# Eight PSUM banks in the ring, and the attention's output summed over head pairs in SBUF

## What is computed

```python
h   = layernorm(x)
# 1: causal attention, 16 heads of 64
qkv = h @ W_qkv + b_qkv
a   = softmax(Q K^T / 8 + causal) V        # per head
a   = a @ W_out + b_out                    # sum over 16 heads = 8 pairs of heads
# 2: two layers of a local transformer, 8 heads of 64, window 64
for l in range(2):
    q, k, v = split(shift(y) @ wqkv[l])    # q, k: l2norm, scale, rotary (x8 on q)
    y = y + local_attention(q, k, v) @ wo[l]
    y = y + (a_ * gelu(g)) @ w2[l] + b2[l] # a_, g from layernorm(shift(y)) @ w1[l]
out = x + a + y
```

## Time and profile before

| | |
|---|---|
| median of 3 runs | 3653.97 us (3653.33 to 3658.05) |
| the profiled execution | 3660.12 us, its span 3658.1 us |
| busy share of the span | PE 87%, DVE 53%, ACT 47%, POOL 28% |
| granted TensorE clock, mean | 0.977 |
| one pass of the loop | 225.0 to 227.9 us, mean 226.4 |

### The profile page before, as it was taken

One profiled execution on the slowest core, in us unless ns is written; L12 is line 12 of the kernel. 1 busy time (PEld: TensorE's weight loads), 2 busy tenths in 40 slices (PEclk: granted clock), 3 DMA queues, 4 the chain that ended last, 5 costly groups with the idle time before them and its releaser, 6 DMA issues.

```text
span 3658.1 us, 95074 instructions
## 1 busy us (share of the span) xinstructions
PE 3187.2 (87%) x34560; PEld 2107.2 (58%) x34560; DVE 1923.1 (53%) x6830; ACT 1704.6 (47%) x3140; POOL 1007.9 (28%) x987
## 2 busy tenths in 40 slices
PE   6888888888888898888988889888898888988897
PEld 4555565555655555555655556555565565555655
DVE  5554554546546464464645546455464464645544
ACT  4444444544444454444544445444454444444543
POOL 4140422404224041240413305133051330513221
PEclk9999999999999999999999999999999999999999
DMA  3000000000000000000000000000000000000000
GB/s 83 8 2 4 8 2 11 2 5 8 2 11 2 5 8 2 11 2 5 8 2 11 2 11 2 2 11 2 11 2 2 11 2 11 2 2 8 2 7 4
DMA packets 41905, 26.37 MB, mean 7 GB/s; under 512 B 13058, under 2 KB 40620, under 8 KB 41388
## 3 DMA queue, kind: packets, MB, share of 16 engines
q1 hardware_dynamic: 41388, 19.56, 1.9%
HBM read 14.96 MB, written 4.19 MB: 5 GB/s over the span
## 4 chain that ended last, share of the span: by engine, by line
PE 64%; issue 10%; DVE 9%; POOL 7%; ACT 4%; DVEq 0%; POOLq 0%; ACTq 0%
PE bank L1175 6%; PE bank L1221 6%; PE bank L1090 6%; PE bank L1207 4%; PE bank L1269 4%; PE bank L1083 3%; POOL rnorm L712 3%; PE bank L1286 3%; PE bank L1251 3%; PE bank L1199 3%; PE bank L1233 2%; PE bank L1309 2%; PE bank L1319 2%; PE bank L1084 2%; PE bank L1085 2%
## 5 line engine op out<-in xcount | busy, mean ns | idle before, releaser
L940 DVE CUSTOM_DVE_ANT_0 bank<-bank,future 128x128 f32<-128x128 f32 (+3 forms) x1024 | 467.9, 527 | 262.6 <-PE bank L1135 262.1
L955 DVE CUSTOM_DVE_ANT_0 bank<-bank,band 128x192 f32<-128x192 f32 x1024 | 330.7, 394 | 248.8 <-PE bank L1154 247.2
L712 POOL TENSOR_TENSOR rnorm<-ssc,minus_half 128x8 f32<-128x8 f32 x256 | 426.5, 1666 | 21.3
L1175 PE MATMUL bank<-Qa,Ka 64*128 64x512 f32 (+3 forms) x2048 | 397.7, 472 | 2.7 <-DVE scratch L997 2.7
L793 ACT ACTIVATE probs<-bank 128x512 f32<-128x512 f32 (+1 forms) x768 | 347.5, 532 | 106.3 <-PE bank L1184 104.7
L1221 PEld LDWEIGHTS bank<-Va,probs 128*64 128x64 f32 x10240 | 327.8, 141 | 104.0 <-issue 88.9
L994 DVE TENSOR_TENSOR scratch<-bank,rope_t 128x512 f32<-128x512 f32 x256 | 176.2, 688 | 355.0 <-ACT scratch L826 217.2
L1221 PE MATMUL bank<-Va,probs 128*64 128x65 f32 x10240 | 361.6, 228 | 0.1
L701 POOL TENSOR_TENSOR lrstd<-lvar,minus_half 128x4 f32<-128x4 f32 x32 | 32.4, 1012 | 1181.6 <-DVE lvar L1018 1181.6
L826 ACT ACTIVATE scratch<-bank 128x512 f32<-128x512 f32 x256 | 153.1, 598 | 437.9 <-PE bank L1269 321.6
L710 POOL TENSOR_SCALAR ssc<-ss 128x8 f32<-128x8 f32 x256 | 95.1, 372 | 855.4 <-DVE ss L1002 843.4
(11 more groups left out here) (153 smaller groups left out, 7011.1 us busy)
## 6 DMA issues: line engine op xcount, KB each, us to landing
x_res<-in_L_attn_x SPq DMA_DIRECT2D x16, 256.0 KB, 2.9
x_rows<-in_L_attn_x SPq DMA_DIRECT2D x16, 256.0 KB, 3.2
out<-yT SPq DMA_DIRECT2D x16, 256.0 KB, 2.3
Lqkv<-in_L_ffn_wqkv SPq DMA_DIRECT2D x2, 768.0 KB, 5.1
rope_t<-in_rope SPq DMA_DIRECT2D x8, 128.0 KB, 4.9
Kf<-in_L_attn_W_qkv SPq DMA_DIRECT2D x1, 768.0 KB, 7.8
Qf<-in_L_attn_W_qkv SPq DMA_DIRECT2D x1, 768.0 KB, 9.4
Lw<-in_L_ffn_w SPq DMA_DIRECT2D x2, 341.0 KB
```

Source lines behind the costliest of these rows:

```text
L712: g.tensor_tensor(rnorm[s][:, :], ssc[:, :], minus_half[:, :], ALU.pow).then_inc(rnorm_ready.sem, 1)
L940: ins = v.tensor_tensor_reduce(psum.bank(i, task, (u, j))[:, at:at + n], psum.bank(i, task, (u, j))[:, at:at + n], future[:, SEQ - n:SEQ], ...
L955: ins = v.tensor_tensor_reduce(psum.bank(i, task, (u, j))[:, k * BAND:(k + 1) * BAND], psum.bank(i, task, (u, j))[:, k * BAND:(k + 1) * BAND],
L1175: mm(bank[j][:, at:end], Ka[p % 2][HALF[j], tile(k)], Qa[p % 2][HALF[j], queries], start=True, stop=False)
```

## The change

- `RING` is 8: every bank belongs to the ring, also in the planner.
- `a_out` claims a bank of the ring for every pair, and its matmul stands alone (`start` and `stop` both set). DVE reads it: for p = 0 it writes bank + bias into the new tile aT_sum, for p = 1 to 6 it adds the bank to aT_sum in place, for p = 7 it writes bank + aT_sum into aT. Before each of these it waits for its own last one (through the read semaphore of that bank), and for p = 7 for the previous `out` on PE, as `a_end` did.
- `a_end`, `out_acc` and the semaphores out_ready and aT_ready are gone. `a_ot` on ACT waits until the last `a_out` filled its bank, where it waited for out_ready; `out` on PE waits until DVE has read the bank of a_out(7).
- The planner has `a_out` with a step of 0.75 on DVE and one bank, and makes a new order.

```diff
-RING = 7
+RING = 8
 BANKS = {...
+         "a_out": 1, ...
-    "a_out": (0.85, [], 0),
-    "a_end": (0.0, [("dve", 0.75, 0.0)], 0),
+    "a_out": (0.85, [("dve", 0.75, 0.0)], 1),
...
-                    elif kind == "a_end":
-                        psum.wait_filled(dve, i, ("out",), "t", before_it(i, task, ("out",)))
-                        dve.sem_inc(carried["dve"], 1)
-                        dve.wait_ge(out_ready.sem, out_ready.now(i, ("a_out", PAIRS - 1), "a"))
-                        v.tensor_scalar(aT, out_acc[:, :], bout[:, 0:1], None, ALU.add).then_inc(aT_ready.sem, 1)
+                    elif kind == "a_out":
+                        p = task[1]
+                        if p == 0:
...
+                            psum.raise_read(v.tensor_scalar(aT_sum, psum.bank(i, task, "u")[:, :], bout[:, 0:1], None, ALU.add), i, task, "u")
+                        else:
+                            other = ("a_out", p - 1)
+                            psum.wait_read(dve, i, other, "u", before_it(i, task, other))
+                            dve.sem_inc(carried["dve"], 1)
+                            if p == PAIRS - 1:
+                                psum.wait_filled(dve, i, ("out",), "t", before_it(i, task, ("out",)))
+                                dve.sem_inc(carried["dve"], 1)
+                            psum.wait_filled(dve, i, task, "u")
+                            psum.raise_read(v.tensor_tensor(aT if p == PAIRS - 1 else aT_sum, psum.bank(i, task, "u")[:, :], aT_sum, ALU.add), i, task, "u")
...
-                        if p == 0:
-                            pe.wait_ge(aT_ready.sem, aT_ready.value(i, ("a_end",), "a", before_it(i, task, ("a_end",))))
-                        mm(out_acc[:, :], Wout[:, p, :], OaT[:, :], start=(p == 0),
-                           stop=(p == PAIRS - 1)).then_inc(out_ready.sem, 1)
+                        bank = psum.claim(pe, i, task, "u")
+                        psum.raise_filled(mm(bank[:, :], Wout[:, p, :], OaT[:, :], start=True, stop=True), i, task, "u")
...
                     elif kind == "out":
-                        pe.wait_ge(aT_ready.sem, aT_ready.now(i, ("a_end",), "a"))
+                        other = ("a_out", PAIRS - 1)
+                        psum.wait_read(pe, i, other, "u", before_it(i, task, other))
+                        pe.sem_inc(carried["pe"], 1)
```

More of the change, by code:

```diff
@@ L52 @@
            ("f_v", 3), ("f_qt", 3), ("f_kt", 3)]
-RING = 7
+RING = 8
 BANKS = {"f_first": 1, "a_proj": 2, "a_v": 1, "a_neg": 1, "a_ot": 1, "f_q": 1, "f_k": 1, "f_v": 1, "f_qt": 1, "f_kt": 1, "f_neg": 1, "f_ot": 1,
-         "f_wo": 1, "f_mean": 1, "f_var": 1, "f_rep": 1, "f_gate": 3, "f_up": 1, "f_down": 1, "out": 1, "xt": 1,
+         "a_out": 1, "f_wo": 1, "f_mean": 1, "f_var": 1, "f_rep": 1, "f_gate": 3, "f_up": 1, "f_down": 1, "out": 1, "xt": 1,
          "a_max": 6, "f_max": 4, "a_st": 6, "f_st": 4, "a_pv": 1, "f_pv": 1}
@@ L113 @@
 A_BEGUN = [task for r in range(-1, PAIRS // 2) for task in attention_round(r)]
-A_REST = [task for r in range(PAIRS // 2, PAIRS + 1) for task in attention_round(r)] + [("a_end",)]
+A_REST = [task for r in range(PAIRS // 2, PAIRS + 1) for task in attention_round(r)]
 def heavy_tasks(l):
@@ L147, in needs @@
         "a_out": lambda: [("a_ot", *at)],
-        "a_end": lambda: [("a_out", PAIRS - 1)],
         "f_first": lambda: [("norm",)],
@@ L161, in needs @@
         "xt": lambda: [("norm",), ("a_proj", PAIRS - 1), ("a_v", PAIRS // 2 - 1, 1)],
-        "out": lambda: [("f_down", DEPTH - 1), ("a_end",)]}.get(kind, lambda: [])()]
+        "out": lambda: [("f_down", DEPTH - 1), ("a_out", PAIRS - 1)]}.get(kind, lambda: [])()]
 def by_ready_time(streams, rotary, pair):
@@ L237 @@
 assert in_order(("norm",), ("f_first",), ("xt",), ("a_proj", 0)) and in_order(("a_proj", PAIRS - 1), ("xt",))
-assert in_order(("a_v", PAIRS // 2 - 1, 1), ("xt",)) and in_order(("a_end",), ("out",)) and in_order(("a_end",), ("a_out", 0))
+assert in_order(("a_v", PAIRS // 2 - 1, 1), ("xt",)) and in_order(("a_out", PAIRS - 1), ("out",))
 def earlier(i, task, which):
@@ L472, in prenorm_attention_and_local_transformer @@
         aT = sb("aT", [P, SEQ])[:, :]
+        aT_sum = sb("aT_sum", [P, SEQ])[:, :]
         Qf = [sb(f"Qf{l}", [P, LPAIRS, SEQ]) for l in range(DEPTH)]
@@ L507, in prenorm_attention_and_local_transformer @@
                     [sem(f"bank{k}_read") for k in range(RING)], dict(
-            a_proj="qk", a_v="v", a_neg="m", a_ot="o", f_first="h", f_q="q", f_k="k", f_v="v", f_qt="q", f_kt="k", f_neg="m", f_ot="o",
+            a_proj="qk", a_v="v", a_neg="m", a_ot="o", a_out="u", f_first="h", f_q="q", f_k="k", f_v="v", f_qt="q", f_kt="k", f_neg="m", f_ot="o",
             f_wo="w", f_mean="c", f_var="v", f_rep="r", f_gate=(0, 1, 2), f_up="a", f_down="w", out="t", xt="x",
@@ L516, in prenorm_attention_and_local_transformer @@
             a_pv="v", f_pv="v"))
-        out_acc = banks[RING]
         xt_ready = Signal(sem("xt_ready"), dict(xt="x"))
@@ L531, in prenorm_attention_and_local_transformer @@
         qk_ready = Signal(sem("qk_ready"), dict(f_q="q", f_k="k"))
-        out_ready = Signal(sem("out_ready"), dict(a_out="a"))
-        aT_ready = Signal(sem("aT_ready"), dict(a_end="a"))
         own = {
             "act": [xt_ready, lt_ready, squares_ready],
-            "dve": [rec_ready, sums_ready, norm_ready, aT_ready, turned_ready["q"]],
+            "dve": [rec_ready, sums_ready, norm_ready, turned_ready["q"]],
             "pool": [rstd_ready, clip_ready, rnorm_ready, turned_ready["k"], qk_ready],
-            "pe": [out_ready]}
+            "pe": []}
         x_loaded, x_again, stored = (sem(name) for name in ("x_loaded", "x_again", "stored"))
@@ L807, in steps @@
                         t0, prev = earlier(i, task, lambda t: t[0] == "a_out")
-                        act.wait_ge(out_ready.sem, out_ready.value(i, t0, "a", prev))
+                        psum.wait_filled(act, i, t0, "u", prev)
                         alone(i, task, "o", OaT[:, :], psum.bank(i, task, "o")[:, :], ACT.Identity,
@@ L1055, in steps @@
                                                                src[HALF[1], 1:SEQ + 1], ALU.add, ALU.add), i, task, "w")
-                    elif kind == "a_end":
-                        psum.wait_filled(dve, i, ("out",), "t", before_it(i, task, ("out",)))
-                        dve.sem_inc(carried["dve"], 1)
-                        dve.wait_ge(out_ready.sem, out_ready.now(i, ("a_out", PAIRS - 1), "a"))
-                        v.tensor_scalar(aT, out_acc[:, :], bout[:, 0:1], None, ALU.add).then_inc(aT_ready.sem, 1)
+                    elif kind == "a_out":
+                        p = task[1]
+                        if p == 0:
+                            if isinstance(i, int):
+                                dve.wait_ge(params, PARAMS)
+                            other = ("a_out", PAIRS - 1)
[5 more added lines that the diff above has]
+                            other = ("a_out", p - 1)
+                            psum.wait_read(dve, i, other, "u", before_it(i, task, other))
+                            dve.sem_inc(carried["dve"], 1)
+                            if p == PAIRS - 1:
+                                psum.wait_filled(dve, i, ("out",), "t", before_it(i, task, ("out",)))
+                                dve.sem_inc(carried["dve"], 1)
+                            psum.wait_filled(dve, i, task, "u")
+                            psum.raise_read(v.tensor_tensor(aT if p == PAIRS - 1 else aT_sum, psum.bank(i, task, "u")[:, :], aT_sum, ALU.add), i, task, "u")
                     elif kind == "out":
```

## The result

The changed kernel takes **3591.16 us** (3589.43 to 3595.92) against 3656.01 for the kernel before on the same chip: ratio 0.9821, interval 0.98 to 0.9841, so 1.8% faster. The profiled span fell from 3658.1 to 3590.4, by 67.7 us or 4.5 us in each of the 15 passes of the loop. First the page of the kernel after.

The account below looks back on a forecast made before the run. PE sets the pace, with 471 us idle. Steps sum to -5.9 us a pass, -4.6 after adds, -2.9 after a clock fall; times 15 passes, -44, giving 3610. Whole range 3555 to 3680; the forecast's own 3590 to 3647.

Parts of the forecast that it names:

- start of a pass: First rotary tasks of a pass: a_out3's add delays f_q(0,0) by 0.7 us, 0.35 remains by f_kt(0,0); +0.2 us a pass.
- front of layer 0: a_max7 to f_kt(0,3): the 2.16 us bank wait goes, new waits 1.6 and 1.2 come; -1.4 us a pass.
- local attention of layer 0: a_max0 takes six banks shortly before f_st(0,3) wants four: 0.8 us new bank waits, 0.2 gone; +0.6 a pass.
- middle: f_mean to f_kt(1,3): 5.5 us of waits before, 3.2 after, with 3.0 at f_kt(1,3); -2.3 us a pass.
- layer 1's attention: f_neg(1,0), f_st(1,0), f_max(1,1) lose waits; f_neg(1,1) gains about 1.0 us, a_st1's exponentials 1.3; -0.7 a pass.
- wait before `out`: End of pass: `out` directly follows f_down(1), costing +1.9 us; 4.2 of other waits go, so -2.3 a pass.
- loop turn: Jump to the next pass: bank 0 about 1.1 us late, hidden by the turn's 3.02 us; nothing gained or lost.
- clock, one more fall at the end: End of pass: idle before and after `out` makes PE's clock fall once more; +1.7 us a pass.
- adds beyond this: Further cost of the DVE adds ahead of reductions: between 0 and 4.8 us a pass, taken as 1.3.
- The signs of being wrong: Loop turn over 3.3 us, PE waits for DVE's maxima (L1135, L1162 <- L940) over 2 us a pass, or clock below 0.96.
- the slower one: Rival: adds land on rotary and maximum chains, each costing its full 0.7 us; +1.1 a pass, 3671 us; chance 0.25.
- Waits move away entirely: Rival: bank waits vanish, no clock fall at the end or f_qt(0,3); 3570 us, or 3585 avoiding only the end's; chance 0.24.

Follow-up runs that it names:

- a second set of seven: Changed kernel with each of the seven two-tensor adds preceded by one more of the same size from the same bank, into a spare tile: 3595.62 us, ratio 0.9831.
- the one with `out` covered: Changed kernel with a_neg4 and the second a_pv3 moved between f_down(1) and `out`, which stays last: 3557.42 us, ratio 0.9735.

## Why the prediction held, and where it didn't

Forecast 3610 with the range 3555 to 3680, faster with 0.67; measured 3591. The main idea holds: the matmuls and VectorE's mean load don't set the time, and the order made anew is most of what pays (3613 without the bank and the adds). The number is closer than the working behind it, since the steps below miss in both directions. By its steps, us a pass, for the pass shown:

| step | predicted | measured |
|---|---|---|
| start of a pass: waits at f_qt(0,0), f_kt(0,0) | +0.2 | about 0: 1.38 and 1.41 before, 1.57 and 1.07 after |
| front of layer 0: waits at f_qt(0,3), f_kt(0,3) | 1.6 and 1.2 | 1.73 and 0.86 |
| local attention of layer 0: new bank waits | 0.8 | 0.81 at a_max0 |
| middle: wait at f_kt(1,3) | 3.0 | 4.09 |
| layer 1's attention: wait at f_neg(1,1) | about 1.0 | 1.89 |
| wait at f_neg(1,2) | not in the sum | 1.26 |
| the exponentials of a_st1 | 1.3 | 0.48 and 0.30 at a_max2 |
| wait before `out` | about 1.9, by the 1.70 of the last sequence | 1.70 |
| f_mean, f_gate, a_max7's bank | gone | gone |
| loop turn | 0 | -1.4 (3.2 to 1.8) |
| clock, one more fall at the end | +1.7 | at most 0.3: PE busy +4.7 us in all |
| adds beyond this | +1.3 | not measured by itself; a second set of seven: 0.3 |

**Right.** The chain lengths read from single rows (6.1 us for q, 6.9 for k) put the two waits of the front within 0.4 us. The wait before `out` was read off the one sequence that had this order already.

**Too small.** f_kt(1,3): the chain itself was as long as counted (6.6 us from the first rotary multiply to kn), but it began 17.9 us after f_wo instead of 13.1, and PE was there 3.5 later than counted too. In the maxima of layer 1, f_neg(1,1) was 0.9 short and f_neg(1,2) was left out. Against these stand the exponentials of a_st1, counted too high. At the steps "Middle" and "Layer 1's attention" the sum was about 2 us a pass too good.

**Misread.** The 0.7 of L1135 behind the exponentials at a_max4 isn't in the row: it has 0.5 at most. The signs of being wrong asked for late maxima of `a_max` only (L940); those of `f_max` came to 53.8 us, 3.6 a pass, and would have been the sign to name.

**Wrong: "Loop turn ... Nothing."** I asked only whether bank 0 would be late, and the turn ended with the wait for it in 4 of 14 passes (5.0 us together). I took the 3.02 as fixed. It isn't: it depends on what stands last, as `out` last in the kernel before shows (-22 us).

**Wrong: the fall of the clock at the end.** I took from one row that the clock stays at 1.00 behind the loop turn, and so counted the end of the pass as a new place for a fall. That row is one of five such turns. In the other nine of the kernel before the clock was at its lower level as PE resumed or within 1.4 us of it, and in the changed kernel behind none of the 14; there it fell during `out` in 2 passes. A turn of each, with the clock behind it (busy times of the engines, then the granted clock before the last two columns), the kernel before first:

```profile
826.85 0.79 PE L1083 MATMUL bank<-xT_hi,Wqkv_hi 128*128 128x512 f32 x1 [3.04 <-issue]
826.50:829.50 3.00, 2.65 (x6) 1.84 (x6) 1.42 (x9) 1.08 (x2) 0.27 (x1) 0.50 0.04 8
...
587.53 0.49 PE L1092 MATMUL bank<-xT_hi,Wqkv_hi 128*128 128x512 f32 x1 [2.12 <-issue]
587.50:592.00 4.50, 4.47 (x38) 2.90 (x40) 1.72 (x11) 2.76 (x4) 1.01 (x1) 1.00 0.15 48
```

So the end of the pass lost falls and gained almost none. They came at a place that the sum didn't have: behind f_neg(1,1)'s 1.89 us the clock fell in 14 of 15 passes. Behind f_kt(1,3) it fell in all 15, as assumed, and behind f_qt(0,3) in 7. Over the whole span the falls about balance (PE busy +4.7 us), which the sum got wrong by 1.7 a pass. The Trainium skill's warning (TensorE: Matmul & The Clock Gate, HAM oscillation) that returning gaps start the next work cold did not decide at the new end of the pass, and did at others. The clock in a stretch behind the 4.09 us wait, and behind the 1.70 in the pass shown:

```profile
2043.80:2051.30 7.50, 3.44 (x7) 1.91 (x8) 0.61 (x1) 2.33 (x5) 3.74 (x3) 0.72 0.01 2
...
2137.00:2138.00 1.00, 1.00 (x6) 1.00 (x6) 0.00 (x0) 0.00 (x0) 0.00 (x0) 0.50 0.06 16
```

The pass shown is one of the two with a fall at `out`; there the matmuls of `out` take 1.6 us longer, and the gap behind them is 0.78 instead of 2, so the fall costs less than its own length.

**Of the rivals**, the slower one named the right mechanism for another kernel: adds cost 31 us when they are put into the old order. In the new order with eight banks even a second set costs 4.5 at most; with seven, adds and their banks cost 27. That the adds are cheap because the order was planned with them is argued and not shown. "Waits move away entirely" was closer than the forecast in its milder form (3585, without the fall at the end), and by a reason of its own, since that fall stayed away in 12 of 14 passes. The forecast's sum without the fall, -4.6 a pass, is as good as the measured -4.5, and that is luck: it leaves out the loop turn's 1.4 and carries 1.3 for adds, against the 2 missed in the middle. The Trainium skill (Perfetto Trace Analysis, Optimization Strategy) says that a gap that returns can mean too few buffers. The bank is worth 48 us in the new order, and the runs agree with it there; in the old order the returning 2.16 only moved one task on.

**Open.** Why the granted clock fell so much more often in the old order with eight banks (0.962), when PE's idle time is only 8 us more. Behind the new waits of 1.4 to 1.6 for the maxima it fell in most passes, but a run in which these alone are filled was not made. Nor was one that moves the adds within the old order, nor one of the first set of adds alone in the new one. Why PE's matmuls are busy longer with seven banks in the new order is open too.

## What to carry to other kernels

A planned order is part of every resource change: test the order alone, the resource alone and both, since here the same exchange was worth -38, +22 and +28 us in three orders. Rank PE's waits by position in one pass and fill each with independent matmuls that stand just behind it; two moves of one to three tasks gave more than the bank did (80 us against 48), and about half of that was idle time and half a higher clock. Where one chain stands behind two waits, filling the first only lengthened the second. And read a place in every pass before a rule is made of it: the one turn of the loop that was read here was not like most of the others.

## What the runs showed of the hardware

- The loop turn's cost on PE depends on the work before it: 3.2 us behind some 80 short matmuls of a_pv, 1.8 to 2.1 behind the 16 of `out` (in the kernel before with `out` last, the changed kernel, and the one with `out` covered). That PE's instructions are issued ahead of the array by that much at `out` would explain it, but was only argued.
- The granted clock fell behind waits much shorter than the loop turn, and not behind all alike: behind 1.89 us at f_neg(1,1) in 14 of 15 passes, behind 2.16 at a_max7 in 9 of the 14 passes of the kernel before that have it, behind 1.70 before `out` in 2 of 16.
- PE's busy time followed the clock when only the order was changed: 3191.9 at 0.975, 3168.6 at 0.981, 3151.6 at 0.985, 3139.8 at 0.990. An estimate from the mean clock (the time at half speed is twice 1 - clock of the span, and half of it is lost) gives 22 of the first 23.3 us. It is no such measure across the resources: the new order with seven banks has 3205.4 at 0.977, the kernel before 3187.2 at the same 0.977.
- Eight more VectorE instructions of 0.69 us a sequence cost 31 us in the old order; seven more cost 4.5 us at most in the new one.
